# One-hot matrices of a graph layer: one comparison a burst in place of 18 or 20

## The reference, cut to what matters

```python
def _L0_gnn_ref(x, edge_index, ...):
    src, dst = (edge_index[0], edge_index[1])
    agg = jax.ops.segment_sum(x[src], dst, num_segments=N)
    h = jax.nn.relu(agg @ W_rel + b_rel + x @ W_root)
    gates = h @ W_ih.T + b_ih + b_hh
    i, f, g, o = jnp.split(gates, 4, axis=-1)
    c = jax.nn.sigmoid(i) * jnp.tanh(g)
    h_lstm = jax.nn.sigmoid(o) * jnp.tanh(c)
    return h_lstm @ W_fc + b_fc
...
x = x + _L0_gnn_ref(_layernorm(x, axis=-1), edge_index, ...)
x = x + _L0_ffn_ref(_layernorm(x, axis=-1)[None], ...)[0]
```

## Time and profile before

| | |
|---|---|
| median of 3 runs | 1309.71 us (1306.66 to 1309.84) |
| span of the profiled execution | 1305.9 us |
| busy, share of the span: PE / PEld | 92% / 81% |
| DVE / ACT / POOL | 62% / 47% / 64% |
| first and last gather start | 69.7 us, 1140.5 us |
| bursts of one-hots, first and last instruction start | 85.0 us, 1124.6 us |

### The profile page before, as it was taken

One profiled execution on the slowest core, in us unless ns is written; L12 is line 12 of the kernel. 1 busy time (PEld: TensorE's weight loads), 2 busy tenths in 40 slices (PEclk: granted clock), 3 DMA queues, 4 the chain that ended last, 5 costly groups with the idle time before them and its releaser, 6 DMA issues.

```text
span 1305.9 us, 25399 instructions
## 1 busy us (share of the span) xinstructions
PE 1195.5 (92%) x8519; PEld 1062.2 (81%) x8519; DVE 814.4 (62%) x2352; ACT 609.5 (47%) x1225; POOL 841.4 (64%) x883
## 2 busy tenths in 40 slices
PE   1066998999999999999999999999999999999998
PEld 0064887988888888888888888888988888898798
DVE  5662455675667656766666566756675667546665
ACT  4721335454544455444535454545444554455432
POOL 3467777777777777777777777777777777700000
PEclk9986999999999999999999999999999999999999
DMA  7764345445544454445444554455444544423399
GB/s 237 258 211 119 111 125 146 137 115 146 145 137 127 131 145 135 135 122 145 144 129 121 144 145 135 115 145 146 136 119 138 145 136 132 127 67 95 109 333 288
DMA packets 127895, 191.81 MB, mean 147 GB/s; under 512 B 55661, under 2 KB 88403, under 8 KB 127819
## 3 DMA queue, kind: packets, MB, share of 16 engines
q0 software_dynamic: 41008, 111.77, 29.6%
q1 hardware_dynamic: 74852, 57.47, 15.5%
q10 hardware_dynamic: 11979, 21.94, 5.0%
HBM read 159.02 MB, written 32.92 MB: 147 GB/s over the span
## 4 chain that ended last, share of the span: by engine, by line
POOL 45%; PE 28%; issue 16%; ACT 3%; DVE 3%; DMA 3%; SPq 1%; POOLq 0%; DVEq 0%; ACTq 0%
POOL ring L658 45%; PE ps L344 6%; PE ps L346 6%; PE ps L345 6%; PE ps L1019 3%; PE ps L1120 2%; DMA ring<-in_x 1%; DMA table<-ring 1%; ACT ps L782 1%; ACT L764 1%; PE ps L1108 1%; ACT x L772 1%; PE ps L965 1%; ACT ring L721 1%; DVE oneh L1454 0%
## 5 line engine op out<-in xcount | busy, mean ns | idle before, releaser
L658 POOL DMA_INDIRECT ring<-table,sidx x851 | 812.8, 955 | 268.8 <-issue 268.5
L344 PE MATMUL ps<-h_h,wih_h 128*128 128x256 f32 x1200 | 346.2, 289 | 0.0
L345 PE MATMUL ps<-h_l,wih_h 128*128 128x256 f32 x1200 | 339.6, 283 | 0.0
L346 PE MATMUL ps<-h_h,wih_l 128*128 128x256 f32 x1200 | 339.4, 283 | 0.0
L1019 PE MATMUL ps<-ring,oneh 128*125 128x512 f16 x974 | 231.3, 383 | 14.3 <-DMA ring<-table,sidx 14.2
L344 PEld LDWEIGHTS ps<-h_h,wih_h 128*128 128x128 f32 x1200 | 229.7, 191 | 3.5 <-issue 0.4
L345 PEld LDWEIGHTS ps<-h_l,wih_h 128*128 128x128 f32 x1200 | 229.9, 192 | 1.7
L346 PEld LDWEIGHTS ps<-h_h,wih_l 128*128 128x128 f32 x1200 | 229.7, 191 | 0.0
L797 ACT ACTIVATE gate<-ps,bgate 128x256 f32<-128x256 f32 x300 | 125.5, 471 | 205.4 <-PE ps L346 204.4
L1019 PEld LDWEIGHTS ps<-ring,oneh 128*125 128x125 f16 x974 | 132.0, 138 | 82.6 <-DMA ring<-table,sidx 21.7
L1454 DVE TENSOR_SCALAR oneh<-iota,rel 128x125 f16<-128x125 f16 x974 | 166.5, 285 | 1.8
(11 more groups left out here) (227 smaller groups left out, 2504.9 us busy)
## 6 DMA issues: line engine op xcount, KB each, us to landing
ring<-table,sidx POOLq DMA_INDIRECT x851, 2.8
swt_d<-swt ACTq DMA_DIRECT2D x25, 500.0 KB
gate<-swt_d SPq DMA_DIRECT2D x19, 500.0 KB, 5.8
table<-ring SPq DMA_DIRECT2D x11, 512.0 KB, 7.0
xn<-table SPq DMA_DIRECT2D x25, 224.0 KB
xin<-in_x SPq DMA_DIRECT2D x25, 224.0 KB
res<-xin SPq DMA_DIRECT2D x25, 224.0 KB
ring<-in_x SPq DMA_DIRECT2D x9, 512.0 KB, 6.9
```

What stands on the lines that cost most here:

```text
L344: eng.matmul(dst, wh, xh, start=first, stop=False)
L345: eng.matmul(dst, wh, xl, start=False, stop=False)
L346: return eng.matmul(dst, wl, xh, start=False, stop=last)
L658: pool.indirect_dma_start(ring[:, j, :], None, table, bass.IndirectOffsetOnAxis(ap=sidx[:, odd * SLOTS + j:odd * SLOTS + j + 1], axis=0)). ...
```

## The change

The offsets `rel` are held in float16 in place of float32 (they are whole numbers; one that is too large for float16 to hold exactly is still far from 0 to 124). The loop of 18 or 20 `tensor_scalar` instructions becomes one `tensor_tensor` over 128 x n x 125 elements: its first operand is `iota`, repeated n times; its second is `rel`, each of its n columns repeated 125 times (a step of 0 in the innermost dimension). Both lie in SBUF, and so does the result. What is waited for and what is signalled stays as it was.

```diff
-        rel = sb("rel", [P, 2 * HOTS])
+        rel = sb("rel", [P, 2 * HOTS], F16)
...
                 dve.tensor_scalar(rel[:, first:first + n], didx[:, idx:idx + n], base, None, ALU.subtract).then_inc(rel_sem, 1)
                 dve.wait_ge(rel_sem, rel_n)
-                for j in range(first, first + n):
-                    last = dve.tensor_scalar(oneh[:, j, 0:WN], iota[:, 0:WN], rel[:, j:j + 1], None, ALU.is_equal)
-                last.then_inc(hot_sem, 1)
+                dve.tensor_tensor(oneh[:, first:first + n, 0:WN], iota[:, 0:WN].unsqueeze(1).to_broadcast([P, n, WN]),
+                                  rel[:, first:first + n].unsqueeze(2).to_broadcast([P, n, WN]),
+                                  ALU.is_equal).then_inc(hot_sem, 1)
```

## The result

The changed kernel takes 1419.75 us (median of 4 runs, 1416.01 to 1420.98), the kernel before 1308.85 us in the same session: a ratio of 1.084 with a 95% interval of 1.083 to 1.086. The forecast was 1410 us with a range of 1376 to 1440. The span of the profiled execution is 1418.5 us against 1305.9.

A forecast was written before the change was run, and what follows sets the result against it. POOL's gathers were taken to bound the kernel, with PE nearly level. Span 1305.9 + 103 for held gathers - 1.5 - 1.5 = 1406 us, plus 3.8 us to the median: 1410 us, range 1376 to 1440.

The forecast's parts named there:

- The bound: POOL's gathers run without slack for 1071 of 1306 us, so a POOL delay goes into the time nearly one for one.
- The length: The new DVE comparison takes 2.75 us for 20 one-hots and 2.49 us for 18, at one element in 1.04 ns.
- The hold: One POOL gather a burst waits for the DVE comparison's end, and itself ends 0.82 us after that.
- The three short cases of the earlier trace: Gathers under L1409, L1676 and the pair L1536 ended 0.82 or 0.83 us after those DVE instructions ended.
- The size of the hold: POOL loses each comparison's length less 0.625 us on the mean, over 50 bursts: 103 us, between 72 and 134.
- What comes back: Gains of 1.5 us from the old bursts' cost to gathers and 1.5 us at the end, where PE was late.
- The clock: PE's clock left at 1.00, with PE waiting some 4 us of 47, split over several blocks.
- the 100 that I had announced: PE's wait for gathered rows was to rise by some 100 us, from 4.4 us.
- the 3.8 us added to the span: The median lies 3.8 us over the profiled span, taking 1406 us of span to 1410 us.
- Double rate: Rival: DVE compares two elements a step, holds of 1.46 and 1.33 us, 1347 us in all; chance 0.07.
- POOL not held: Rival: gathers slip in under the new DVE comparison, 1308 us, no measurable difference; chance 0.06.
- Longer than reckoned: Rival: the new DVE comparison takes as long as the old burst, 135 us lost, 1442 us; chance 0.05.

The follow-up runs named there:

- e2_ts16: Kernel before with its 18 or 20 small comparisons, only the offsets put in half precision: 1309.05 us, ratio 1.001.
- pieces of four: Changed kernel with each burst's single comparison split into comparisons of four one-hots each: 1346.88 us, ratio 1.031 to the kernel before.
- e8_phase: Changed kernel with a one-input maximum over 384 elements added between the subtraction and the comparison: 1401.94 us, ratio 1.072 to the kernel before.
- the run with the maximum in every burst: Kernel before with an unread one-input maximum over 2500 or 2250 elements added ahead of each burst's small comparisons: 1346.78 us, ratio 1.030.
- the one on the slow chip: Two-input comparisons of one one-hot, every fifth by the old one-input kind, 32-bit offsets: 1782.97 us against 1903.78 for the kernel before there, ratio 0.939.
- e1_f32: Changed kernel with its offsets back in 32 bits, one comparison a burst kept: 1418.89 us, ratio 1.086 to the kernel before.
- pieces of two: Changed kernel with each burst's single comparison split into comparisons of two one-hots each: 1317.04 us, ratio 1.007 to the kernel before.

## Why the prediction was right, point by point

**The bound** (POOL has no slack, so its losses go into the time): right. From the first to the last start the gathers need 1251.1 - 69.5 = 1181.6 us against 1070.8; the difference of 110.8 us is all but 1.8 us of the span's. In the runs above the span follows the gathers' busy time: 812.1 and 1306.2 us (e2_ts16), 853.4 and 1343.7 (pieces of four), 909.2 and 1400.1 (e8_phase), 923.6 and 1418.5. Only the run with the maximum in every burst leaves this line, for the reason found, and the one on the slow chip. What the forecast says of a gain of POOL, that 13.3 us of it would go in, counts PE's 8.9 us of waits for ACT too, which faster gathers wouldn't shorten; no run made use of it.

**The length** (2.75 and 2.49 us): right, 2.77 and 2.50 us, the single rate. In the bound at double rate "1250 x 0.52" should read 2500 x 0.52; the 1.30 us behind it is right.

**The hold** (one gather a burst, to the end and 0.82 us more): right, 50 of 50. The three short cases of the earlier trace rows told it.

**The size of the hold** (length less 0.625 us, in all 103 us): this term was 6 us too small. The holds are 109.3 us, so the mean offset was 2.70 - 2.19 = 0.51 us. The step that failed is "0 to 1.25 us after the instruction's start, on the mean 0.625": neither the bounds nor the even spread are right, and the two errors partly cancel, which was luck.

The bounds first. A gather that reaches its point just behind the start of a two-input instruction still goes free. Timelines of POOL and of DVE, 617 to 621 us, in the changed kernel:

```profile
617.36 0.95 POOL L658 DMA_INDIRECT ring<-table,sidx  x1 [0.30 <-issue]
618.61 2.36 POOL L658 DMA_INDIRECT ring<-table,sidx  x1 [0.30 <-issue]
...
617.34 2.82 DVE L1453 TENSOR_TENSOR oneh<-iota,rel 128x2500 f16<-128x2500 f16 x1
```

The first reaches its point 0.15 us after the comparison's start and isn't held; the second, one pitch later, waits to the end. The kernel before shows where the edge lies: there 94 gathers reach their point up to 0.16 us after the start of an instruction with two SBUF inputs and lose 0.08 us at most, and 24 reach it at 0.165 us or later and each lose just what is left of the instruction, to within 0.02 us. So the held one arrives 0.17 to 1.42 us after the start, on the mean 0.79 if phases were even, and that would have cost 135 - 50 x 0.79 = 95 us (an estimate). Behind an unbroken row of two-input instructions the edge is earlier: the gather of 665.41 us above was 0.10 us behind the start of its row.

The phases then are not even. 31 of the 50 comparisons start 0.03 to 0.04 us after a gather's end, 0.27 us before the next gather's start, and lose their length less 0.40 us. What puts them there is the subtraction ahead of them: when it starts 0.28 to 0.43 us before a gather's end, it ends with the gather, as in the rows of 536 us, and the comparison follows. One that starts at other places takes its usual 0.23 us. The old kernel had this too. Beside the gather of 607.16 in the earlier trace rows, which ends at 608.19, stood this row of DVE's timeline, which ends there as well:

```profile
607.88 0.31 DVE L1451 TENSOR_SCALAR rel<-didx,wbase 128x20 f32<-128x20 int32 x1
```

In 23 of the 50 bursts of before the subtraction ended with a gather. I had the row in view when I reckoned with even phases.

**What comes back** (1.5 us for the old bursts, 1.5 at the end): wrong in sign, 6 us together. What isn't in the 50 long gathers is 1181.6 - 850 x 1.25 - 109.3 = 9.8 us against 8.3 before. The old bursts' 2.0 us did come back, but the other two-input instructions met more gathers in the new rhythm: L1510 cost them 2.3 us and nothing before, L1604 2.4 and 0.7. And from the last gather's start to the end it is 167.4 us, 2.0 more than before, where the forecast had 1.5 less. PE no longer came late to the last sums: it waited three times for them.

```profile
1251.78 0.86 PE L1019 MATMUL ps<-ring,oneh 128*125 128x512 f16 x3 [0.71 <-DMA ring<-table,sidx]
1253.16 0.43 PE L1019 MATMUL ps<-ring,oneh 128*125 128x512 f16 x1 [0.53 <-DMA ring<-table,sidx]
1254.55 0.69 PE L1019 MATMUL ps<-ring,oneh 128*125 128x512 f16 x1 [0.96 <-DMA ring<-table,sidx]
```

**The clock** (left at 1.00): wrong, and without a price in the turns. The mean is 0.950 against 0.988. In every second turn PE waits twice for rows, here 2.7 us up to 400.84 and 3.2 us up to 406.01, and about the end of the first wait (here at 400.7) the granted clock falls to 0.50 (1.2 of 2.4 GHz) for 6.8 or 10.2 us. The changed kernel in stretches (length; PE, PEld, DVE, ACT, POOL busy; granted clock, DMA share, GB/s):

```profile
395.00:400.60 5.60, 3.16 (x24) 2.63 (x23) 4.51 (x10) 4.55 (x11) 4.08 (x6) 1.00 0.36 103
400.60:410.80 10.20, 6.76 (x20) 4.79 (x21) 2.44 (x7) 1.58 (x3) 7.76 (x9) 0.50 0.40 122
```

This is why PE's wait for rows is 63.6 us and not the 100 that I had announced: PE is busy for 1236.1 us in place of 1195.5, 41 us more for the same instructions. It had to wait for POOL anyway, and POOL never waited for it. Nor do the 2 us at the end follow from the lower clock: the change with 32-bit offsets (e1_f32) has the same three waits behind its last gather, 2.0 against 2.2 us, and the same 3.4 us at the lower clock, and yet 165.4 us to the end, as before the change. Where the 2 us of the profiled execution come from stays open.

The errors together, 6 for the holds and 6 for what comes back, are the 12 us between 1406 and the span of 1418.5. The forecast of the median was off by less, 10 us, because a third error took 2.5 us back: the 3.8 us added to the span. Each run's time is 1.8 to 1.9 us over its own span, and the median is 1.3 us over that of the profiled one; the rest of the 3.8 was the spread of the first runs. This too was luck.

**The rivals.** Double rate: not here, but real, 1.48 us and 1356 us once the offsets are stored in pairs (1347 was reckoned). POOL not held: refuted by the 50 held gathers, and by all runs with long instructions of two inputs. Longer than reckoned: no. Where POOL is the bound, no version with two-input comparisons beats the kernel before; pieces of two, with half as many instructions, come nearest and are 0.7% slower.

## What to carry to other kernels

Where POOL issues indirect DMAs without slack, count the DVE instructions with two SBUF inputs that are longer than the gathers' pitch, and add up their lengths, less some 0.2 us each: that is the most that they can cost, and the share of DVE's idle time says nothing about it. Fewer instructions are only better if the one that replaces them doesn't read a second input from SBUF: the 20 one-input comparisons took longer on DVE (3.40 against 2.77 us) and cost POOL almost nothing. If two inputs can't be avoided there, pieces of about 0.4 us were far cheaper (0.7% slower than before) than one piece of 2.8 us (8.4%), and also than many of 0.28 us (9.2%).

## What the runs showed of the hardware that I had not expected

- A row of two-input instructions of 0.28 us, started 0.20 us apart, shuts out to the row's end a gather that comes 1.39 us or more after the row's start (waits up to 2.74 us); rows of 0.42 us at 0.33 us don't (0.16 us at most). One one-input instruction in between lets a waiting gather in, but a gather that comes behind it can be shut out at once (0.78 us at 1.07 us into the burst).
- A gather that reaches its point up to 0.16 us after the start of a two-input instruction goes free (94 in the kernel before, 0.08 us lost at most, packed rows aside); from 0.165 us on it waits for the end.
- A gather can delay DVE too, and that locks phases: the one-input subtraction of 0.23 us (L1451), started 0.28 to 0.43 us before a gather's end, ends with the gather (0.28 to 0.44 us long), and what follows starts at a fixed place in the gather's cycle. 31 of 50 comparisons did.
- 20 us more work for DVE made a kernel 18 us faster, by moving a two-input instruction past the point at which a gather can be held.
